# The turn of a slot's second-layer result placed between the two halves of the next slot's first-layer turn

## The chip, the cores and the metric

The kernel runs on one core of one Trainium2 chip. The metric is the device time of one execution in microseconds; the time shown for the kernel before is the median of 3 runs.

## The reference

Three residual blocks over x of 64 x 32 tokens with 256 channels: cross-attention to 257 context rows of 192 channels with 16 heads, local attention with a window of two tokens to each side, and a routed feed-forward part. The change touches the last one alone:

```python
router_logits = x @ Wr + br                       # 2048 tokens, 8 experts
expert_mask = one_hot(argmax(router_logits))      # one expert for each token
for e in range(8):
    h = gelu(x @ W1[e] + b1[e])                   # 256 -> 1024
    h = gelu(h @ W2[e] + b2[e])                   # 1024 -> 512
    y = h @ W3[e] + b3[e]                         # 512 -> 256
    out = out + expert_mask[:, e:e + 1] * y
```

## The kernel before

Both attention parts run over tiles of 128 tokens and end near 435 us. Then the tokens are sorted by expert into 23 slots of 128 rows (`SLOTS`), each slot with one expert, and each slot goes through three matrix layers. Every fp32 product is made of three products of rounded parts (`PRODUCTS`: high by high, high by low, low by high).

The work is written out for each engine, and semaphores join them. Each engine works its list in order. `over_slots` runs five slots straight, then a loop of three rounds of five slots, then the last three straight.

**PE**, for slot i (`slot`, L1810): layer 2 of slot i (24 matmuls, L1748), the turn of x for slot i+2 (2 transposes, L1687), the turn of z1 for slot i+1 (two halves of 4 transposes, L1728), the turn of z2 for slot i (4 transposes, L1756), layer 1 of slot i+2 (12 matmuls, L1696), layer 3 of slot i (13 matmuls, L1770 and L1762). z1 and z2 are the results of layers 1 and 2 with a token on each partition; a turn brings the channels onto the partitions, for the activation with its bias and for the next layer.

**ACT**, for slot i (`slot`, L958): copy of z2 from PSUM (`copy_z2`, L885), copies of the turned x (L870, L871), the second activation with its rounding for slot i (`second_layer`, L930 and L934; it waits for the turn of z2), the first activation with its rounding for slot i+1 in two halves (`first_layer`, L894 and L898; each half waits for its half of the turn of z1), the copies of z1 for slot i+2 (L876), the copy of y (L881). In the slot before the last, `first_layer_last` (L907, L911) comes ahead of `second_layer`.

**GpSimd (POOL)** makes the low parts: of x (L710), of the second layer's input (L717) and of the third's (L721); it also adds the residual (L727) and issues the gathers and scatters. **DVE** splits the weights into parts as they come in (L1336, L1339). **SP** issues their transfers, each as soon as the layer that reads the buffer's old contents has run for the last slot of its expert.

The waits around the change, on PE: the turn of z2 waits for `z2_copied` (ACT, L885) and `h2_hi_done`; each half of the turn of z1 waits for `z1_copied` (ACT, L876) and `h1_hi_done`; layer 2 waits for `h1_hi_done`, the rounding by L898, half by half. The halves of the turn of z1 go to the banks `ps_s[2]` and `ps_s[0]`, the turn of z2 goes to `ps_s[3]`, and layer 2 writes `ps_s[1]`.

Of the kernel before, what the change touches and what calls it, by code (L numbers as in the profile page):

```python
# [20 lines left out]
def perceiver_kernel(nc, x, ctx_turned, last_turned, mask, Wq, Wk, Wv, Wo, lWq_turned, lbq, lWk_turned, lbk, lWv, lbv,  # L21
# [30 lines left out]
    with ExitStack() as stack:  # L52
# [342 lines left out]
        def follows(i, n):  # L395

            return not isinstance(i, int) or i + n < SLOTS
# [7 lines left out]
        def is_last(i):  # L405
            return isinstance(i, int) and i == LAST
# [950 lines left out]
        def _(pe):  # L1357
# [58 lines left out]
            def keep_clock(n):  # L1416

                for _ in range(n):
                    t.transpose(ps_s[0][:, 0:P], ident[:, :], ident[:, :])
# [303 lines left out]
            def turn_z1_half(i, half):  # L1723
                pe.wait_ge(z1_copied, 2 * i + half + 1)
                pe.wait_ge(h1_hi_done, 2 * i)
                for c in range(4):
                    f = 4 * half + c
                    last = t.transpose(ps_t1[half][:, c * P:(c + 1) * P], z1[:, f * P:(f + 1) * P], ident[:, :])  # L1728
                last.then_inc(t1_filled, 1)

            def turn_z1(i):
                for half in range(2):
                    turn_z1_half(i, half)

            def layer2(i, e):
                pe.wait_ge(z2_copied, i)
                for products in (PRODUCTS[0:2], PRODUCTS[2:3]):
# [14 lines left out]
            def turn_z2(i):  # L1752
                pe.wait_ge(z2_copied, i + 1)
                pe.wait_ge(h2_hi_done, i)
                for c in range(F2 // P):
                    last = t.transpose(ps_t2[:, c * P:(c + 1) * P], z2[:, c * P:(c + 1) * P], ident[:, :])  # L1756
                last.then_inc(t2_filled, 1)
# [8 lines left out]
            def layer3_hi(i, e):  # L1766
                pe.wait_ge(w23_ready, 3 * e + 3)
                pe.wait_ge(h2_hi_done, i + 1)
                pe.wait_ge(y_copied, i)
                t.matmul(ps_y[:, 0:D], ones_r[:, :], b3_parts[:, bass.ds(e * D, D)], start=True, stop=False)  # L1770
                layer3_products(e, PRODUCTS[0:2], range(F2 // P))

            def layer3_lo(i, e):
                pe.wait_ge(h2_done, i + 1)
                layer3_products(e, PRODUCTS[2:3], range(F2 // P)).then_inc(y_filled, 1)
# [18 lines left out]
            def load_expert(i, q):  # L1794
                pe.reg_load(expert_in[q], slot_expert_int[0:1, bass.ds(i, 1)])

            def expert_of(q):
                return pe.snap(expert_in[q], min_val=0, max_val=E - 1)
# [11 lines left out]
            def slot(i, run, q):  # L1810
                expert = expert_of(q)
                layer2(i, expert)
                if is_last(i):
                    other = postponed.pop()
                    layer3_hi(i - 1, other)
                    turn_z2(i)
                    layer3_lo(i - 1, other)
                    keep_clock(8)
                    layer3_last(expert)
                    return  # L1820
                if follows(i, 2):
                    load_expert(i + 2, (q + 2) % AHEAD)
                    ahead = expert_of((q + 2) % AHEAD)
                    turn_x(i + 2, run + (q + 2) // AHEAD, (q + 2) % AHEAD)
                if follows(i, 1):
                    turn_z1(i + 1)
                turn_z2(i)
                if follows(i, 2):
                    layer1(i + 2, ahead)
                if last_but_one(i):  # L1830
                    postponed.append(expert)
                else:
                    layer3(i, expert)
# [38 lines left out]
```

## Time and profile before

| | |
|---|---|
| median of 3 runs | 742.54 us (741.34 to 744.79) |
| the profiled execution | 742.61 us |
| its span, first to last instruction | 740.9 us |
| mean granted TensorE clock | 0.987 |
| PE busy | 707.6 us, 96% |
| PE weight loads busy | 601.9 us, 81% |
| DVE busy | 470.0 us, 63% |
| ACT busy | 452.7 us, 61% |
| POOL busy | 422.7 us, 57% |

The share of the busy time is an average over parts of the kernel with different limits. Times in the rows further down are microseconds from the start of the span. PE stands for matmuls, PEld for the weight loads that run ahead of them; a transpose is a matmul too, with its load. The ends of matmuls are modelled, so PE can look busy while it waits, and the starts of the loads tell more.

### The profile page before, as it was taken

How to read it: one execution, taken by the hardware profiler on the slowest of the kernel's cores; microseconds unless marked ns; L12 is line 12 of the kernel's file. 1: busy time of each engine (PE TensorE's matmuls, PEld its weight loads, DVE VectorE, ACT ScalarE, POOL GpSimd, SP SyncE). 2: the span in 40 equal slices, each digit the busy share in tenths (PEclk: the TensorE clock that was granted, in tenths of full speed). 3: DMA queues.
4: the chain of work that ended last, by engine and by line, in shares of the span. 5: the costliest groups of instructions: out<-in, count | busy, mean ns of one | idle time of the engine just before them, and what ended most of it. 6: DMA issues, size and time to landing. Idle time of an engine off the chain costs nothing.

```text
span 740.9 us, 26310 instructions
## 1 busy us (share of the span) xinstructions
PE 707.6 (96%) x9211; PEld 601.9 (81%) x9212; DVE 470.0 (63%) x1381; ACT 452.7 (61%) x1073; POOL 422.7 (57%) x562
## 2 busy tenths in 40 slices
PE   8999999999999999999999848999999999997995
PEld 7888888888888888888888737887888888886884
DVE  4466677667776777777776569969923880288000
ACT  4666666666666666676666254565665757564654
POOL 6466656565565555555654104575757776675553
PEclk9999999999999999999999988999999999998999
DMA  7222332324232333334332903256026422271000
GB/s 219 89 79 83 82 89 78 92 65 105 78 90 66 79 96 83 80 74 92 86 81 95 341 29 100 93 180 223 22 100 211 145 79 78 86 256 36 21 7 1
DMA packets 55439, 73.92 MB, mean 100 GB/s; under 512 B 6269, under 2 KB 41118, under 8 KB 55392
## 3 DMA queue, kind: packets, MB, share of 16 engines
q1 hardware_dynamic: 49248, 60.36, 27.9%
q0 software_dynamic: 2944, 8.13, 3.6%
q10 hardware_dynamic: 3200, 4.80, 1.8%
q8 instruction: 29, 0.48, 0.3%
q14 instruction: 18, 0.15, 0.1%
HBM read 66.90 MB, written 7.27 MB: 100 GB/s over the span
## 4 chain that ended last, share of the span: by engine, by line
PE 84%; DVE 9%; DMA 3%; ACT 1%; issue 1%; POOL 0%; SPq 0%; POOLq 0%; ACTq 0%; DVEq 0%
PE ps_s L1748 15%; PE ps_kv L1366 11%; PE ps_kv L1374 11%; PE ps_p L1413 7%; PE ps_o L1399 6%; PE ps_s L1385 5%; DVE w L1339 3%; PE ps_kv L1696 3%; PE ps_p L1696 3%; PE ps_o L1762 3%; DVE w L1336 2%; PE ps_m L1512 2%; PE ps_m L1465 2%; PE ps_m L1444 2%; PE ps_s L1728 2%; PE ps_m L1517 2%
## 5 line engine op out<-in xcount | busy, mean ns | idle before, releaser
L1007 DVE CUSTOM_DVE_ANT_0 prob<-ps_s,mask_add 128x257 f32<-128x257 f32 x256 | 94.8, 422 | 66.8 <-PE ps_s L1385 66.8
L780 ACT ACTIVATE prob<-prob,neg_max 128x257 f32<-128x257 f32 x256 | 111.2, 500 | 41.7 <-DVE neg_max L1007 40.2
L1339 DVE TENSOR_TENSOR w<-w_raw,w 128x512 fp32r<-128x512 f32 x112 | 105.3, 943 | 3.7
L1336 DVE CAST w<-w_raw 128x512 fp32r<-128x512 f32 x94 | 63.4, 674 | 69.0 <-DMA w_raw<-in_L_ffn_W_dram 69.0
L612 POOL TENSOR_TENSOR ctx_parts<-ctx_raw,ctx_parts 128x512 fp32r<-128x512 f32 x64 | 82.8, 1293 | 31.5 <-ACT ctx_parts L775 30.5
L1748 PE MATMUL ps_s<-w,h_hi 128*128 x368 | 93.7, 406 | 7.2 <-DVE w L1339 5.9
L1748 PEld LDWEIGHTS ps_s<-w,h_hi 128*128 128x128 f32 x368 | 68.5, 191 | 25.5 <-issue 10.4
L1366 PE MATMUL ps_kv<-ctx_parts,wkv_hi 128*128 128x256 f32 x512 | 85.7, 295 | 0.2 <-POOL ctx_parts L612 0.2
L1374 PE MATMUL ps_kv<-wkv_hi,ctx_parts 128*128 128x256 f32 x512 | 84.9, 293 | 1.0 <-ACT kT L784 1.0
L717 POOL TENSOR_TENSOR h_lo<-h,h_hi 128x512 fp32r<-128x512 f32 x46 | 65.0, 1413 | 25.3 <-ACT h_hi L898 20.6
L788 ACT COPY v<-ps_kv 128x512 f32<-128x512 f32 x64 | 37.5, 585 | 66.6 <-PE ps_kv L1374 66.6
L1413 PE MATMUL ps_p<-ident,prob 128*128 128x128 f32 x512 | 77.0, 273 | 0.8 <-DVE probT L1029 0.8
L1366 PEld LDWEIGHTS ps_kv<-ctx_parts,wkv_hi 128*128 128x128 f32 x512 | 71.0, 191 | 2.3 <-issue 0.4
L1374 PEld LDWEIGHTS ps_kv<-wkv_hi,ctx_parts 128*128 128x128 f32 x512 | 69.4, 189 | 3.4 <-ACT kT L784 1.9
L605 POOL TENSOR_TENSOR ctx_raw<-ctx_raw,last_ctxT 128x512 f32<-128x512 f32 x64 | 69.4, 1085 | 1.3 <-DMA ctx_raw<-in_ctx_turned_dram 1.3
L1029 DVE COPY probT<-ps_p 128x512 f32<-128x512 f32 x64 | 44.1, 689 | 36.4 <-PE ps_p L1413 34.9
L885 ACT COPY lqk<-ps_s 128x512 f32<-128x512 f32 x23 | 13.5, 586 | 82.6 <-PE ps_s L1748 82.6
L1413 PEld LDWEIGHTS ps_p<-ident,prob 128*128 128x128 f32 x512 | 60.2, 141 | 2.9 <-DVE probT L1029 1.0
L625 POOL COPY last_prob<-prob 128x4 f32<-128x4 f32 x64 | 12.0, 187 | 87.7 <-ACT prob L780 80.6
L784 ACT COPY kT<-ps_kv 128x512 f32<-128x512 f32 x64 | 37.3, 582 | 28.0 <-PE ps_kv L1366 27.9
L894 ACT ACTIVATE h<-ps_s,bias_cols 128x128 f32<-128x128 f32 x176 | 50.1, 367 | 4.8 <-issue 3.9
L1399 PEld LDWEIGHTS ps_o<-v,probT 128*32 128x32 f32 x4096 | 41.0, 110 | 12.9 <-issue 12.6
(259 smaller groups left out, 1534.6 us busy)
## 6 DMA issues: line engine op xcount, KB each, us to landing
w_raw<-in_L_ffn_W_dram SPq DMA_DIRECT2D x24, 1024.0 KB, 7.8
ctx_raw<-in_ctx_turned_dram SPq DMA_DIRECT2D x63, 256.0 KB, 3.6
mask_add<-mask_dram SPq DMA_DIRECT2D x64, 128.5 KB, 3.4
rows_dram<-x3n ACTq DMA_DIRECT2D x16, 256.0 KB, 4.3
w_raw<-in_L_ffn_W_dram SPq DMA_DIRECT2D x8, 512.0 KB, 5.1
xt<-in_x_dram SPq DMA_DIRECT2D x16, 128.0 KB, 2.0
xr<-in_x_dram SPq DMA_DIRECT2D x16, 128.0 KB, 2.2
slot_x<-rows_dram,slot_ids POOLq DMA_INDIRECT x23, 3.7
```

What stands on the lines that cost most here:

```text
L605: g.tensor_tensor(ctx_raw[:, b, :, :], ctx_raw[:, b, :, :], last_ctxT[:, :, bass.ds(n, 1)].to_broadcast([P, 2, JM]), ALU.subtract).then_in ...
L612: g.tensor_tensor(ctx_parts[:, b % 2, 2:4, :], ctx_raw[:, b, :, :], ctx_parts[:, b % 2, 0:2, :].bitcast(F32), ALU.subtract).then_inc(split ...
L717: g.tensor_tensor(h1_parts[LO][:, fs, :], h1[:, fs, :], h1_parts[HI][:, fs, :].bitcast(F32), ALU.subtract).then_inc(h1_done, 1)
L780: a.activation(prob[:, g, :], prob[:, g, :], ACT.Exp, bias=neg_max[:, g:g + 1], scale=-1.0).then_inc(exp_done, 1)
L1007: d.tensor_tensor_reduce(prob[:, r, :], ps_s[r][:, 0:J], mask_add[:, k, :], -(HD ** -0.5), 3.0e38, ALU.add, ALU.min, neg_max[:, r:r + 1]). ...
L1336: d.tensor_copy(w[:, b, HI, part], raw[:, b, part]).then_inc(rounded, 1)
L1339: last = d.tensor_tensor(w[:, b, LO, part], raw[:, b, part], f32(w[:, b, HI, part]), ALU.subtract)
L1366: last = t.matmul(ps_kv[:, half * JM:(half + 1) * JM], w[:, 0, r, half * P:(half + 1) * P], ctx_parts[:, buffer, c, :], start=(i == 0), st ...
L1374: last = t.matmul(ps_kv[:, jt * D:(jt + 1) * D], ctx_parts[:, buffer, c, jt * P:(jt + 1) * P], w[:, 1, r, :], start=(i == 0), stop=(i == 4))
L1399: last = t.matmul(ps_o[h * S:(h + 1) * S, g * BLOCK:(g + 1) * BLOCK], probT[:, jt, g * P + h * S:g * P + (h + 1) * S], v[:, k % 2, jt, g / ...
L1413: last = t.transpose(ps_p[:, g * P:(g + 1) * P], prob[:, g, jt * P:(jt + 1) * P], ident[:, :])
L1748: last = t.matmul(ps_z2[:, :], h1_parts[hp][:, f, :], weight(w23, e % BUFFERS23, wp, f * F2, F2), start=(hp == HI and wp == HI and f == 0) ...
```

## The change

In PE's list for a slot, the turn of z2 of slot i moves up by four transposes: it now stands between the first and the second half of the turn of z1 of slot i+1. The function that did both halves in a row is dropped. The last slot and all other engines' lists stay as they are.

```diff
-            def turn_z1(i):
-                for half in range(2):
-                    turn_z1_half(i, half)
-
...
                 if follows(i, 1):
-                    turn_z1(i + 1)
+                    turn_z1_half(i + 1, 0)
                 turn_z2(i)
+                if follows(i, 1):
+                    turn_z1_half(i + 1, 1)
                 if follows(i, 2):
                     layer1(i + 2, ahead)
```

## Rows read from the trace of the kernel before

**Rows 1.** The page, chain that ended last, shares of the span by engine.

```profile
PE 84%; DVE 9%; DMA 3%; ACT 1%; issue 1%; POOL 0%; SPq 0%; POOLq 0%; ACTq 0%; DVEq 0%
```

**Rows 2.** Line L1756: its instructions, and who waited for it (us, times).

```profile
L1756 PEld LDWEIGHTS ps_s<-ident,lqk x92: 139/140/143, 466.6 to 730.5; 128*128 128x128 f32 x92
...
  ACT x3n L930: 12.7, 21
```

**Rows 3.** Order of time, PE's loads, one slot: start, us, what [idle before].

```profile
620.78 0.90 PEld L1728 LDWEIGHTS ps_s<-ident,prob 128*128 128x128 f32 x8
621.65 0.47 PEld L1756 LDWEIGHTS ps_s<-ident,lqk 128*128 128x128 f32 x4
622.09 0.77 PEld L1696 LDWEIGHTS ps_p<-w,xT_hi 128*128 128x128 f32 x4
...
623.37 0.89 PEld L1696 LDWEIGHTS ps_kv<-w,xT_hi 128*128 128x128 f32 x4
...
625.95 0.55 PEld L1762 LDWEIGHTS ps_o<-w,h_lo 128*128 128x128 f32 x4
626.65 0.52 PEld L1748 LDWEIGHTS ps_s<-w,h_hi 128*128 128x128 f32 x3 [0.16 <-issue]
```

**Rows 4.** Order of time, ACT, the same slot.

```profile
620.87 0.58 ACT L885 COPY lqk<-ps_s 128x512 f32<-128x512 f32 x1 [3.25 <-PE ps_s L1748]
...
622.59 1.14 ACT L930 ACTIVATE x3n<-ps_s,bias_cols 128x128 f32<-128x128 f32 x4 [0.58 <-PE ps_s L1756]
...
625.75 0.62 ACT L898 CAST h_hi<-h 128x512 fp32r<-128x512 f32 x1
```

**Rows 5.** Order of time: transposes behind a wait, and in a full stream.

```profile
455.66 0.60 ACT L876 COPY prob<-ps_p 128x512 f32<-128x512 f32 x1
...
456.31 0.42 PEld L1728 LDWEIGHTS ps_s<-ident,prob 128*128 128x128 f32 x4 [0.73 <-ACT prob L876]
...
456.32 0.66 PE L1728 MATMUL ps_s<-ident,prob 128*128 128x128 f32 x4 [0.29 <-ACT prob L876]
...
621.76 0.60 PE L1756 MATMUL ps_s<-ident,lqk 128*128 128x128 f32 x4
```

**Rows 6.** Order of time, PE's loads, a slot in which POOL held one up.

```profile
657.18 0.77 PEld L1696 LDWEIGHTS ps_p<-w,xT_hi 128*128 128x128 f32 x4
658.43 0.30 PEld L1696 LDWEIGHTS ps_p<-w,xT_lo 128*128 128x128 f32 x2 [0.48 <-POOL xT_lo L710]
658.77 0.88 PEld L1696 LDWEIGHTS ps_kv<-w,xT_hi 128*128 128x128 f32 x4
...
661.35 0.55 PEld L1762 LDWEIGHTS ps_o<-w,h_lo 128*128 128x128 f32 x4
661.82 0.31 PEld L1748 LDWEIGHTS ps_s<-w,h_hi 128*128 128x128 f32 x2
```

**Rows 7.** Order of time, ACT, a slot with a longer idle before L930.

```profile
540.14 1.14 ACT L930 ACTIVATE x3n<-ps_s,bias_cols 128x128 f32<-128x128 f32 x4 [0.87 <-PE ps_s L1756]
```

**Rows 8.** Order of time, PE's first loads of layer 2, outside the loop.

```profile
703.49 3.56 PEld L1748 LDWEIGHTS ps_s<-w,h_hi 128*128 128x128 f32 x16
...
715.08 1.00 PEld L1748 LDWEIGHTS ps_s<-w,h_hi 128*128 128x128 f32 x5
```

**Rows 9.** Order of time, ACT and PE's loads, into the last slot.

```profile
720.99 0.59 ACT L885 COPY lqk<-ps_s 128x512 f32<-128x512 f32 x1 [3.26 <-PE ps_s L1748]
...
723.07 0.39 PEld L1748 LDWEIGHTS ps_s<-w,h_hi 128*128 128x128 f32 x2 [1.02 <-issue]
```

**Rows 10.** The chain that ended last, in order of time: start, us, what.

```profile
644.21 5.55 DMA w_raw<-in_L_ffn_W_dram
...
680.05 5.96 PE ps_s L1748 x16
```

**Rows 11.** Busy time by stretch: us, each engine (instructions), granted clock, DMA share, GB/s.

```profile
511.00:580.00 69.00, 68.64 (x371) 57.96 (x371) 42.30 (x56) 43.45 (x122) 45.91 (x41) 1.00 0.31 103
676.00:680.00 4.00, 0.00 (x0) 0.00 (x0) 3.90 (x7) 0.14 (x1) 3.54 (x4) 0.70 0.10 32
680.00:686.00 6.00, 5.95 (x18) 4.69 (x19) 2.05 (x4) 0.00 (x0) 0.08 (x1) 0.63 0.10 31
```

## The prediction

> **What bounds the kernel now.** The page is read first: the chain that ended last is PE for most of the span [rows 1]. The change touches only the routed part, which starts near 450 us, so the views of that part come next. The list of who waits for the turn of the second-layer result shows 92 transposes, 23 slots of four, and that in 21 of the slots it is ACT that waits for them, before the activation at L930 [rows 2]. The order of time on PE's weight loads is then read over one slot, and the order of time on ACT over the same slot [rows 3, 4].
>
> The two together show a loop through both engines. Layer 2's first load comes at 614.96 in the slot before and 626.65 in this one, a period of 11.69 us (the first of these is one period ahead of the row shown). Inside it: the copy of z2 (L885) starts at 620.87, the activations of L930 at 622.59 after ACT was idle for 0.58 us on L1756, the first cast of L898 starts at 625.75 and ends at 626.37, and PE's load for layer 2 comes 0.28 us later, at 626.65, after 0.16 us of idle [rows 3, 4]. The same 0.28 us, give or take 0.02, stands between the end of that cast and this load in nearly every slot. So it is ACT that sets the period, by a little, while PE looks full.
>
> How little: in this slot the distance from the loads of layer 3's last product to layer 2's is 0.70 us (625.95 to 626.65) [rows 3]. In a slot in which PE had just been held up it is 0.47 us (661.35 to 661.82) [rows 6]. PE thus has 0.23 us of slack, and its own period would be 11.69 - 0.23 = 11.46 us.
>
> **The change, part by part.** Nothing is removed or added: the same twelve transposes of a slot run in another order, with the same waits. No DMA and no step of SP, POOL or DVE moves.
>
> *The turn of z2 comes earlier.* Its first load is at 621.65, after eight loads 0.11 us apart from 620.78 [rows 3]. With only four ahead it could start at 621.21. But it waits for the copy of z2, which ends at 620.87 + 0.58 = 621.45 [rows 4]. What the wait costs after that is in a place where PE waits for a copy of ACT: the copy ends at 455.66 + 0.60 = 456.26 and the load starts at 456.31, 0.05 us later [rows 5]. So the load starts at 621.50: 0.15 us earlier than now, and 0.29 us later than PE could take it. **A wait that the second half of the z1 turn covered until now is laid bare.**
>
> *What it costs PE.* The queue behind that wait is the second half of the z1 turn, then layer 1, layer 3 and layer 2 of the next slot. Not all of the 0.29 us is lost: four transposes that start on an idle array end 0.67 us after their first load (456.31 to 456.98), four in a full stream 0.71 us after (621.65 to 622.36) [rows 3, 5]. The stream behind moves by 0.29 - 0.04 = 0.25 us. The row gives 0.05 us for the wait.
> The Trainium skill (Advanced Engine Details and Errata, Network/Comms) gives 50 to 100 ns for the reading of a semaphore from a sequencer; the row is at its lower end. By its upper end, which no row here shows for this wait, the shift would be 0.30 us, and by that figure the sum would be about 0.8 us higher.
>
> *What it gives ACT.* The last transpose of z2 would end at 621.50 + 0.67 = 622.17 in place of 622.36, so L930 starts 0.15 us (by the loads) to 0.19 us (by the ends) earlier. ACT had been idle before it, so it can. All that follows on ACT, to the cast of L898, hangs on that start: ACT's part of the loop comes down to 11.50 to 11.54 us.
>
> *The second half of the z1 turn comes later:* its four loads came from 621.21, now they follow the four of z2, from about 622.0. Their reader is the second group of L894, which ACT starts only behind the cast of L898 at 625.75: over three us of cover. It costs nothing.
>
> *The two together.* PE's period becomes 11.46 + 0.25 = 11.71 us and ACT's 11.52. The larger decides: 11.71 against 11.69 now. **ACT's gain is real, and PE cannot take it, since the order that gives it spends PE's slack.** That PE's slack swallows such a delay is in the trace: a load held by POOL for 0.48 us moved the loads behind it from 1.28 us after layer 1's first (622.09 to 623.37) to 1.59 us after (657.18 to 658.77), so by 0.31 us, and the distance before layer 2 shrank from 0.70 to 0.47 us [rows 3, 6].
>
> *Where it counts.* 23 slots are turned. From 644.21 to 680.05 the chain runs through a weight transfer and DVE's rounding of it [rows 10]; three slots' turns lie beside it, and two more beside an earlier chain of that kind (489 to 511). The last two slots have other chains. 23 - 5 - 2 = 16 count. Twelve of them are in the loop of the program. In nine the period is like the one above: 9 x 0.02 = +0.2 us. In three ACT is late for a reason of its own, as at 540.14, where it had been idle for 0.87 us in place of 0.58 [rows 7]; there PE waits for longer than its slack and most of the 0.15 us is taken: 3 x 0.12 = -0.35 us. Four stand outside the loop, where ACT loses less before L894 and the period is down to 11.59 us (703.49 to 715.08) [rows 8]: PE's 11.71 costs up to 0.12 us there, estimated at 0.09 on average, +0.35 us. A POOL hold at layer 1 and the new stall don't add, since the later of the two decides.
> *The last slot.* There is no turn of x ahead; the copy of z2 starts at 720.99 and PE stands idle for 1.02 us before layer 2 at 723.07 [rows 9]. A turn of z1 that is 0.44 us later fits in there: nothing.
>
> Sum: +0.2 - 0.35 + 0.35 = +0.2 us. The profiled execution took 742.61 us with a span of 740.9; the median of the three runs is 742.54. **Forecast: 742.8 us,** the execution's 742.61 and the sum. What a measurement of this kernel can tell from no change is about 0.5%, or 3.7 us.
>
> **The rivals.**
> *PE's stall is paid in full (slower).* One mechanism at one place: the load of z2 waits at the head of PE's queue, and PE's slack of 0.23 us before layer 2 is not slack. Against it: the slack comes from the difference of two distances, and the held slot at 658.43. For it: PE is reported idle for only 0.16 us at that place, not 0.23 [rows 3]. With the stall paid in full, 16 x 0.25 = 4.0 us, 746.6. It turns into a loss as soon as the stall exceeds the slack by 0.02 us a slot; it would be beyond 0.5% only with nearly nothing absorbed. With 0.16 us of slack, it is 16 x 0.09 = 1.4 us, 744.0.
> *ACT's gain comes through (faster).* If the stream behind moves by far less than 0.25 us, because the loads behind catch up, ACT stays the bound and the full 0.15 us a slot is gained: 16 x 0.15 = 2.4 us, 740.1. For it: of the 0.48 us hold only 0.31 came through, so streams do catch up [rows 6]. Against it: the four transposes behind a wait of the same kind got back only 0.04 us [rows 5].
> *The clock.* PE's granted clock was 1.00 over 511 to 580 although each slot has 14 transposes, and 0.63 over 680 to 686, after PE had run nothing from 676 to 680 [rows 11]; 16 matmuls took 5.96 us there where their loads otherwise take 3.56 [rows 8, 10]. If the new gap of 0.3 us among the transposes brought such a fall once or twice, the cost is some 2 us each: 745 to 747.
> The Trainium skill (TensorE: Matmul & The Clock Gate, Part 4: PE-mode transpose) says that transposes do not count as work for the clock gate, which would make a gap among them worse than one elsewhere; the trace's 1.00 over whole slots speaks against it deciding here. By it the time would be that of the rows, 745 to 747.
> *The change does nothing,* because the copy's end and not the order sets the z2 turn already: excluded by 621.45 against 621.65.
>
> **How the numbers follow.** Forecast case (PE and ACT about level, within 1.5 us of now) 0.74; ACT's gain comes through 0.11; the stall is paid in part or in full 0.11, of which a third beyond 0.5%; the clock 0.04. Range 740.2 to 745.8: the lower end is the full gain of ACT, the upper one is most of a stall paid. Faster by over 0.5%: 0.03 (2.4 us plus luck with the clock at 680). Slower by over 0.5%: 0.07. Within 0.5%: 0.90.
>
> **What would show it.** In the changed kernel: the first load of L1756 0.05 us after the end of L885, PE idle there by about 0.2 to 0.3 us with ACT as the releaser; ACT's idle before L930 down from 0.58 to about 0.40; no idle before L1748's first load; the period 11.7. If the period is 11.55 the catch-up was under-rated, if it is above 11.8 the slack was over-rated. A clock below 1.00 between 511 and 644 would make the prediction wrong.

## The result, and the profile after

The changed kernel takes 740.72 us in the median of 18 runs (739.81 to 742.13), the kernel before 742.42 us in 18 runs beside them (739.17 to 745.66). The ratio is 0.9979, with an interval of 0.9969 to 0.9989. So the change gains 1.7 us, 0.2%. The forecast was a loss of 0.2 us. The time lies inside the forecast's range, but it moved in the direction that had got little weight, and the reasons have to be looked at one by one.

The profiled execution of the changed kernel took 740.58 us, with a span of 738.8 against 740.9. The page's head, its first row of engines and the chain that ended last, which answers [rows 1]:

```profile
span 738.8 us, 26310 instructions
PE 708.2 (96%) x9211; PEld 600.4 (81%) x9212; DVE 472.1 (64%) x1381; ACT 453.1 (61%) x1073; POOL 425.7 (58%) x562
PE 88%; DVE 7%; DMA 1%; ACT 1%; issue 1%; POOL 0%; SPq 0%; POOLq 0%; ACTq 0%; DVEq 0%
```

The share of DVE in that chain fell from 9% to 7% and that of DMA from 3% to 1%. Rounded as they are, that is some 15 us of a chain at least that left the path (the one of slot 4, from 489 to 511, is such a chain). The change touches neither engine. This row is the first hint of where the gain is.

In the code of the changed kernel the lines behind L1730 are four lower: L1748 is L1744 now, L1756 is L1752, L1762 is L1758. The turn of z2, the view that answers [rows 2]:

```profile
L1752 PEld LDWEIGHTS ps_s<-ident,lqk x92: 138/140/144, 466.3 to 728.4; 128*128 128x128 f32 x92
...
  ACT lqk L885: 6.1, 23
...
  ACT x3n L930: 8.6, 21
```

ACT waits for these transposes for 8.6 us in place of 12.7, and PE now waits 6.1 us for the copy of z2, 0.26 us a slot on average. The same slot as in [rows 3, 4], in the order of time: PE's loads, then ACT.

```profile
618.80 0.47 PEld L1728 LDWEIGHTS ps_s<-ident,prob 128*128 128x128 f32 x4
619.52 0.42 PEld L1752 LDWEIGHTS ps_s<-ident,lqk 128*128 128x128 f32 x4 [0.26 <-ACT lqk L885]
619.91 0.47 PEld L1728 LDWEIGHTS ps_s<-ident,prob 128*128 128x128 f32 x4
620.35 0.76 PEld L1696 LDWEIGHTS ps_p<-w,xT_hi 128*128 128x128 f32 x4
...
624.20 0.54 PEld L1758 LDWEIGHTS ps_o<-w,h_lo 128*128 128x128 f32 x4
624.66 2.41 PEld L1744 LDWEIGHTS ps_s<-w,h_hi 128*128 128x128 f32 x11
```

```profile
618.88 0.59 ACT L885 COPY lqk<-ps_s 128x512 f32<-128x512 f32 x1 [3.46 <-PE ps_s L1744]
...
620.41 1.15 ACT L930 ACTIVATE x3n<-ps_s,bias_cols 128x128 f32<-128x128 f32 x4 [0.39 <-PE ps_s L1752]
...
623.58 0.62 ACT L898 CAST h_hi<-h 128x512 fp32r<-128x512 f32 x1
```

The load of z2's turn comes 0.05 us after the copy's end (618.88 + 0.59 = 619.47, then 619.52). L930 starts 1.53 us after the copy's start, where it was 1.72. The distance from layer 3's last product to layer 2 is 0.46 us (624.20 to 624.66), where it was 0.70: PE's slack is used up. And the load of layer 2 comes 0.46 us after the end of the cast (624.20), where it was 0.28: **ACT now runs about 0.2 us ahead of PE at the start of layer 2 in most slots** (in a few it has no lead, in some 0.4 us), where PE was right behind ACT before.

So this slot is as forecast. The first loads of layer 2 give a ledger of the slots (before, after):

| first load of layer 2 | before | after | difference | gained between |
|---|---|---|---|---|
| slot 4 | 507.12 | 507.13 | +0.01 | |
| slot 5 | 520.47 | 518.83 | -1.64 | -1.65 in slot 4 |
| slot 16 | 650.06 | 648.08 | -1.98 | -0.34 in slots 5 to 15 |
| slot 18 | 673.49 | 671.76 | -1.73 | +0.25 in slots 16 and 17 |
| slot 19 | 691.82 | 689.57 | -2.25 | -0.52 in slot 18 |
| slot 22 | 723.07 | 721.00 | -2.07 | +0.18 in slots 19 to 21 |

Four fifths of the difference come from one slot. PE's loads of layer 2 in slot 4, first of the kernel before, then of the changed one:

```profile
507.12 1.69 PEld L1748 LDWEIGHTS ps_s<-w,h_hi 128*128 128x128 f32 x8
510.71 1.69 PEld L1748 LDWEIGHTS ps_s<-w,h_hi 128*128 128x128 f32 x8 [1.90 <-issue]
```

```profile
507.13 3.57 PEld L1744 LDWEIGHTS ps_s<-w,h_hi 128*128 128x128 f32 x16
```

Before, PE stopped for 1.90 us in the middle of layer 2. After, the 16 loads run through. What PE waits for there is the second half of W2 of the third expert. Its path: when layer 2 of slot 2 has run (the *trigger*, the start of L885 in that slot, 489.38 before, 489.46 after), SP issues the transfer, and DVE splits the two pieces of W2 into high and low parts in 16 operations (L1336 and L1339 in turn). PE is ready for the second half 19.3 to 19.5 us after the trigger in every kernel below. In the kernel before DVE was done at +21.20, in the changed one at +19.34.

The second place is slot 18, which waits for the last expert's W2. The granted clock there, in the changed kernel, answers [rows 11] (columns: us, PE, PEld, DVE, ACT, POOL busy, granted clock, DMA share, GB/s):

```profile
511.00:580.00 69.00, 68.88 (x373) 57.43 (x372) 43.32 (x55) 45.49 (x126) 47.60 (x41) 1.00 0.33 105
676.00:680.00 4.00, 1.78 (x5) 1.43 (x6) 3.86 (x8) 0.00 (x0) 1.94 (x2) 0.81 0.30 78
680.00:686.00 6.00, 5.98 (x30) 4.85 (x29) 0.28 (x1) 1.84 (x6) 0.73 (x1) 0.84 0.00 0
```

From that slot's trigger (end of layer 2 in slot 15) to the end of DVE's splitting it is 35.7 to 35.8 us in both kernels, so the order gains nothing there. But layer 2 of slot 18 ends 41.5 us after the trigger in place of 41.8, and that of slot 19 starts 47.27 us after it in place of 47.61. Around the end of the stop the granted clock is at the lower of its two levels (1.2 GHz, half) for a while. By these rows and [rows 11] it is (0.19 x 4 + 0.16 x 6) / 0.5 = 3.4 us in the profile of after and (0.30 x 4 + 0.37 x 6) / 0.5 = 6.8 us in that of before. The 6.8 us began some 2.4 us before PE went on at 680.04 (the mean clock was 0.90 over 676 to 678 and 0.50 over 678 to 680).

### The profile page after: what moved, and what is told of

Read it like the earlier page. It is cut to its first block, busy times and chain, and to the rows that moved or that the text cites. A ratio compares the mean times of both kernels' runs of the same rounds, so it can differ in the third digit from the quotient of the medians.

```text
span 738.8 us, 26310 instructions
## 1 busy us (share of the span) xinstructions
PE 708.2 (96%) x9211; PEld 600.4 (81%) x9212; DVE 472.1 (64%) x1381; ACT 453.1 (61%) x1073; POOL 425.7 (58%) x562
## 4 chain that ended last, share of the span: by engine, by line
PE 88%; DVE 7%; DMA 1%; ACT 1%; issue 1%; POOL 0%; SPq 0%; POOLq 0%; ACTq 0%; DVEq 0%
PE ps_s L1744 16%; PE ps_kv L1366 11%; PE ps_kv L1374 11%; PE ps_p L1413 7%; PE ps_o L1399 6%; PE ps_s L1385 5%; PE ps_p L1696 4%; PE ps_kv L1696 4%; PE ps_o L1758 4%; PE ps_s L1728 2%; DVE w L1339 2%; PE ps_m L1512 2%; PE ps_m L1465 2%; PE ps_m L1444 2%; PE ps_m L1517 2%; PE ps_s L1752 2%
## 5 line engine op out<-in xcount | busy, mean ns | idle before, releaser
L1336 DVE CAST w<-w_raw 128x512 fp32r<-128x512 f32 x94 | 70.8, 753 | 65.4 <-DMA w_raw<-in_L_ffn_W_dram 65.4
L1339 DVE TENSOR_TENSOR w<-w_raw,w 128x512 fp32r<-128x512 f32 x112 | 99.9, 895 | 3.7
L1744 PE MATMUL ps_s<-w,h_hi 128*128 x368 | 91.9, 401 | 4.8 <-DVE w L1339 4.3
L1744 PEld LDWEIGHTS ps_s<-w,h_hi 128*128 128x128 f32 x368 | 68.3, 190 | 20.9 <-issue 6.3
L717 POOL TENSOR_TENSOR h_lo<-h,h_hi 128x512 fp32r<-128x512 f32 x46 | 64.5, 1403 | 27.3 <-ACT h_hi L898 22.4
L885 ACT COPY lqk<-ps_s 128x512 f32<-128x512 f32 x23 | 13.5, 586 | 84.5 <-PE ps_s L1744 84.5
L1399 PEld LDWEIGHTS ps_o<-v,probT 128*32 128x32 f32 x4096 | 41.0, 110 | 12.9 <-issue 12.6
```

The lines of the kernel that those rows point to most:

```text
L717: g.tensor_tensor(h1_parts[LO][:, fs, :], h1[:, fs, :], h1_parts[HI][:, fs, :].bitcast(F32), ALU.subtract).then_inc(h1_done, 1)
L1336: d.tensor_copy(w[:, b, HI, part], raw[:, b, part]).then_inc(rounded, 1)
L1339: last = d.tensor_tensor(w[:, b, LO, part], raw[:, b, part], f32(w[:, b, HI, part]), ALU.subtract)
L1399: last = t.matmul(ps_o[h * S:(h + 1) * S, g * BLOCK:(g + 1) * BLOCK], probT[:, jt, g * P + h * S:g * P + (h + 1) * S], v[:, k % 2, jt, g / ...
L1744: last = t.matmul(ps_z2[:, :], h1_parts[hp][:, f, :], weight(w23, e % BUFFERS23, wp, f * F2, F2), start=(hp == HI and wp == HI and f == 0) ...
```

## The experiments

All kernels of this part, those of the order of before and those of the changed order, read the expert's number on PE with stated bounds in place of a plain load of the register:

```diff
-                pe.reg_load(expert_in[q], slot_expert_int[0:1, bass.ds(i, 1)])
+                pe.reg_mov(expert_in[q], pe.value_load(slot_expert_int[0:1, bass.ds(i, 1)],
+                                                       min_val=0, max_val=E - 1))
```

The expectations name theories by letters, and the quoted texts say what each expects. In short: A, the forecast's account, by which the loop is level and what remains is the clock behind slot 18's stop; B, the loop itself gains; C, the stop in slot 4 makes it; D, the weight transfer of slot 4 collides with GpSimd's gather and scatter around the trigger; E, it is how DVE's splitting alternates with GpSimd's work; F, a sharper form of C, by which the lead of ACT and GpSimd over PE at the trigger decides how often PE has to stop.

**Both orders once more.** First the kernel before and the changed one with only the edit above.

> The kernel before, with one thing added: PE loads the expert's number with its bounds asserted (as ACT does), which the experiments with edits need too. It is the base of the experiments. Theory A (the gain lies in when the weights of one expert arrive): the slots in which no weights are waited for have a period near 11.70 us, and the stop of PE before the second half of layer 2 in slot 4 (1.65 us in the trace of before) is there again, though its size may differ from run to run. Theory B (the gain lies in the loop of PE and ACT itself): the same periods, but the stop in slot 4 has no part in the difference to the changed order. Both: a time within 0.5 us of the kernel before, 742.4 us.

> The changed kernel with the same added assertion on PE. Theory A: the plain slots have 11.70 to 11.72 us again, not less than in the base, and slot 4 has no stop or a clearly shorter one; 1 to 2 us faster than the base. Theory A2 (as A, but the arrival of the weights is a matter of chance in each execution): slot 4 may show a stop here as well, and the difference to the base is under 1 us. Theory B: the plain slots are shorter than in the base by 0.1 us each.

Measured: 742.30 us (741.06 to 743.51, 11 runs) and 741.36 us (740.46 to 745.57, 12 runs), against 742.39 of the kernel before (23 runs); ratios 0.9998 (0.9987 to 1.0010) and 0.9987 (0.9975 to 1.0000). No cost of the edit can be seen. Between the two medians lie 0.9 us, in the direction of the gain, but with 11 and 12 runs that is not quite clear of nothing (95% interval from resampling the runs: a loss of 0.1 to a gain of 1.5 us). What these two taught was in their profiles. The order of before had a stop in slot 4 of only 0.18 us this time (profiled run 741.37 us), and the changed order had one of 1.68 us (742.09 us):

```profile
506.43 1.69 PEld L1748 LDWEIGHTS ps_s<-w,h_hi 128*128 128x128 f32 x8 [0.22 <-issue]
508.35 1.70 PEld L1748 LDWEIGHTS ps_s<-w,h_hi 128*128 128x128 f32 x8 [0.23 <-issue]
```

```profile
507.00 1.73 PEld L1744 LDWEIGHTS ps_s<-w,h_hi 128*128 128x128 f32 x8
510.46 1.70 PEld L1744 LDWEIGHTS ps_s<-w,h_hi 128*128 128x128 f32 x8 [1.72 <-issue]
```

So **the stop is not fixed by the order: in either order it can be short or about 1.7 us long.** Profiles further down confirm it for programs that are the same up to slot 4: the order of before has 0.18 us here and 1.89 us in the pair on slot 18, the changed order 1.68 us here and 0.06 us with the first five slots changed. What the order can change is how often.

**No weights to wait for.** The transfers and the splitting of the weights are left out from the fourth expert on for the first layer and from the third on for the others. Later slots then work with the matrices of earlier experts, and no slot waits for weights. DVE signals the buffers as ready by copies of one column.

```diff
             for first_matrix, e in LATE:
+                if e >= (3 if first_matrix else 2):
+                    continue
...
```

> The order of before; the transfers and the splitting of the weights of the later experts (third W1 buffer onward and all W2 and W3 behind the first two experts) are left out, so part of the computation uses the weights of earlier experts, and no slot waits for weights. What is left is PE with ACT and POOL. Both theories: some 6 us or more below the kernel before, since the stops of slots 4 and 18 go (1.65 and 6.6 us). Theory A: about level with its counterpart in the changed order. Theory B: 1.5 to 2 us above it.

> The changed order with the same parts of the weights' transfers and splitting left out. Theory A: within 0.5 us of the order of before without weights, rather above it than below (11.71 against 11.69 and 11.60 us a slot). Theory B: 1.5 to 2 us below it.

Measured: 733.74 us (733.29 to 734.27) and 733.78 us (733.69 to 734.32), four runs each. The medians are level to 0.04 us. With four runs each that holds to some 0.5 us, so the gain of 1.7 us sits on the waits for weights, little or none of it in the loop as such, and theory B fell. The spread of a kernel is at most 1 us here; with the weights it is 1.6 to 6.5 us, in more runs.

**Slot 4 without its wait.** The transfer and the splitting of the third expert's W2 and W3 are left out, and its slots 4 to 8 work with the first expert's matrices.

```diff
             for first_matrix, e in LATE:
+                if not first_matrix and e == 2:
+                    continue
...
```

> The base in the order of before; the transfer and splitting of W2 and W3 of the third expert are left out, so its slots 4 to 8 use the first expert's matrices, and slot 4 waits for no weights. Slot 18's stop stays. Theory A (plain slots level, the gain in the arrival of weights in slot 4 and in the clock after the stop in slot 18): 0 to 1 us below the base, and 0.5 to 1 us above its counterpart in the changed order. Theory C (only slot 4's stop makes the difference): level with its counterpart within 0.3 us.

> The changed order with the same left out. Theory A: 0.5 to 1 us below its counterpart in the order of before, with TensorE at half clock for 3.4 us after slot 18's stop where the order of before has 6.8 us. Theory C: level with it.

Measured: 740.89 us (739.66 to 742.11) and 741.06 us (740.60 to 742.19), 12 runs each, against 742.48. Level: 0.17 us the other way, known to some 0.7 us. Taking the stop away gains 1.4 us in the order of before (from 742.30) and 0.3 in the changed one (from 741.36), which has most of it already; the 0.3 alone is within the noise. Theory C held. The half-clock stretch at slot 18 is still in both kernels, 6.8 us in the profile of the first and 3.4 us in that of the second, and the medians are level all the same. That speaks against the part of theory A that puts the gain there.

**Slot 18 without its wait.** The same for the last expert's W2 and W3 (`e == 7`); its slots 18 to 22 work with the sixth expert's.

> The base in the order of before; the transfer and splitting of W2 and W3 of the last expert are left out (its slots 18 to 22 use the sixth expert's), so that PE does not stop in slot 18 and the clock does not fall there. Slot 4 may stop. Theory A: 6 to 8 us below the base, and above its counterpart by less than 0.8 us (what slot 4 makes). Theory C: above its counterpart by the full 1 to 1.7 us.

> The changed order with the last expert's W2 and W3 left out. Theory A: within 0.8 us of its counterpart, since the clock has no part here. Theory C: 1 to 1.7 us below it.

Measured: 735.75 us (734.16 to 736.79, 6 runs) and 734.80 us (734.32 to 736.03, 5 runs). A difference of 0.95 us remains without slot 18's stop, as large as in the first pair. So few runs can't tell it from nothing (95% interval: a loss of 0.4 to a gain of 1.8 us), and it lies just under theory C's 1 to 1.7 and just over theory A's 0.8. (Both profiles happen to show the long stop in slot 4, 1.89 and 1.75 us.) The stop in slot 18 costs 6 to 7 us in either order.

**The way cleared for the transfer.** GpSimd's gather for slot 5 and scatter of slot 1 are moved away from the trigger.

```diff
-                if i + 3 < SLOTS:
+                if i + 3 < SLOTS and i != 2:
                     gather_slot(i + 3)
-                if i > 0:
+                if i > 0 and i != 2:
                     scatter_slot(i - 1)
...
+                if i == 1:
+                    gather_slot(5)
+                if i == 2:
+                    scatter_slot(1)
```

> The base in the order of before; POOL issues the gather of slot 5 one slot earlier (behind the low part of slot 1's second-layer result), and the scatter of slot 1 behind the low part of slot 2's, so that neither is on its way when the third expert's W2 is called for at the end of slot 2's layer 2. Theory D (slot 4's stop comes from this transfer sharing the DMA engines with a gather and a scatter issued 1.9 and 0.3 us ahead of it; the changed order lets ACT and POOL lead PE by 0.2 to 0.4 us and so frees the way): the transfer lands after 5.5 to 5.9 us, not 6.9 to 7.4; the stop is under 0.3 us; 1 to 1.5 us below the base. Theory E (the stop comes from how DVE's splitting alternates with POOL's work, not from the transfer): the landing may be earlier, the stop stays in most executions; level with the base.

> The changed order with the same move of one gather and one scatter. Theory D: level with e9 within 0.4 us, and 0 to 0.6 us below the changed order, since its stop, where it still comes, goes too. Theory E: 0.8 to 1.5 us below e9, as without the move.

Measured: 744.84 us (742.21 to 745.70, 11 runs) and 744.57 us (742.55 to 746.11, 10 runs), ratios 1.0021 (1.0009 to 1.0033) and 1.0022 (1.0011 to 1.0033): slower than the kernel before (742.41) by 2.4 and 2.2 us in the medians. Neither theory had expected that; D had expected 1 to 1.5 us less and E no change for the first. The two are level with each other, as D had said. The first half of theory D came true as well: the first piece landed at +5.42 and +5.62 us in place of +7.26. But DVE was done later, at +21.8 and +22.2, and the stops in slot 4 were 2.6 and 2.9 us. The trace of the order of before with the way cleared, DVE and then GpSimd, shows why:

```profile
495.74 0.43 DVE L1340 CAST w<-w_raw 128x512 fp32r<-128x512 f32 x1 [3.77 <-DMA w_raw<-in_L_ffn_W_dram]
496.20 4.01 DVE L1343 TENSOR_TENSOR w<-w_raw,w 128x512 fp32r<-128x512 f32 x1
500.14 0.41 DVE L1340 CAST w<-w_raw 128x512 fp32r<-128x512 f32 x1
```

```profile
495.36 1.02 POOL L735 DMA_INDIRECT out_dram<-y,slot_ids  x1 [0.16 <-issue]
496.41 2.56 POOL L717 TENSOR_TENSOR h_lo<-h,h_hi 128x512 fp32r<-128x512 f32 x2
498.94 0.72 POOL L727 TENSOR_TENSOR y<-y,slot_x 128x256 f32<-128x256 f32 x1
```

The moved scatter held GpSimd up, so its two L717 and L727 came back to back. One DVE operation that otherwise takes 0.69 us lasted 4.01 us, until 0.55 us after the end of that row (499.66). That is theory E's point: an operation of DVE that meets one of GpSimd waits for its end, here for the whole row, which had no gap.

**GpSimd made later in the changed order.** One copy of 128x128 more ahead of the gather for slot 5.

```diff
+                if i == 2:
+                    g.tensor_copy(band_shifted[:, :], band[:, :])
                 if i + 3 < SLOTS:
                     gather_slot(i + 3)
```

> The changed order; POOL makes one copy of 128 x 128 more (some 0.5 us) ahead of the gather of slot 5, which takes away its lead there. Theory D: gather and scatter go out as late as in the order of before, the third expert's W2 lands 0.5 to 1.5 us later than in the changed order on average, and the time goes up by about 1 us to 742.2. Theory E: level with the changed order within 0.4 us.

Measured: 741.45 us (739.98 to 743.37, 12 runs), ratio 0.9987 (0.9977 to 0.9997), the same as without the copy (741.36). The scatter started 0.09 us before the trigger in place of 0.87, and the transfer still landed at +5.75. So the place of gather and scatter alone doesn't decide, and theory D, which had expected 742.2, fell.

**PE made later in the order of before,** once, by three transposes ahead of layer 2 of slot 2. ACT and GpSimd then have the lead that the changed order gives them, at this one trigger.

```diff
                                     pe.wait_ge(h1_hi_done, 2 * i + half + 1)
+                                    if isinstance(i, int) and i == 2 and hp == HI and half == 0:
+                                        for _ in range(3):
+                                            t.transpose(ps_s[3][:, 0:P], ident[:, :], ident[:, :])
```

> The base in the order of before; three transposes more on PE (0.3 us) ahead of slot 2's layer 2, so that this one trigger comes 0.3 us later against ACT and POOL, as it does in the changed order. Theory D: the stop of slot 4 gets rarer or shorter; 0.3 us paid, about 1 won: 0.5 to 0.9 us below the base. Theory E: 0 to 0.3 us above the base.

Measured: 741.58 us (740.73 to 743.33, 11 runs), ratio 0.9992 (0.9983 to 1.0000). **With work that does nothing put on the busiest engine, the median is 0.7 us lower** than that of its counterpart without it (742.30), as theory D had expected; the interval of the ratio just reaches no change, so this is support and not proof. PE's loads into slot 2 and in slot 4:

```profile
482.86 0.35 PEld L1750 LDWEIGHTS ps_s<-ident 128*128 128x128 f32 x3
483.18 1.00 PEld L1751 LDWEIGHTS ps_s<-w,h_hi 128*128 128x128 f32 x5
...
506.69 1.70 PEld L1751 LDWEIGHTS ps_s<-w,h_hi 128*128 128x128 f32 x8 [0.27 <-issue]
509.00 1.69 PEld L1751 LDWEIGHTS ps_s<-w,h_hi 128*128 128x128 f32 x8 [0.61 <-issue]
```

The stop is 0.6 us. The comparison is across two groups of runs, each against its own runs of the kernel before (742.39 and 742.41).

**The order changed in some slots only.** Five straight slots at the start alone, and then all slots but these (with the opposite condition in the first line).

```diff
+                apart = isinstance(i, int) and i < AHEAD
                 if follows(i, 1):
                     turn_z1_half(i + 1, 0)
+                    if not apart:
+                        turn_z1_half(i + 1, 1)
                 turn_z2(i)
-                if follows(i, 1):
+                if follows(i, 1) and apart:
                     turn_z1_half(i + 1, 1)
```

> The changed order in the five straight slots at the start alone (slots 0 to 4); the loop of three rounds and the last three slots have the order of before. Theory F (what the change gives is all in the stop of layer 2 in slot 4, and that hangs on how far ACT and POOL lead PE when the weight transfer is triggered, at the end of slot 2's layer 2): the whole difference is here, so 741.0 to 741.4 us against 742.4 of the kernel before, ratio 0.9981 to 0.9987; the outer slots at the end then keep their old period, which is worth another 0.2 us. In the profile the lead before slot 2's layer 2 is 0.45 us or more (0.28 before). Theory A (the loop and the clock at slot 18 make it): level with the kernel before, 742.2 to 742.5.

> The counterpart: slots 0 to 4 have the order of before, the loop and the last three slots have the changed one. Theory F: nothing of the gain is left, 742.2 to 742.7 us, ratio 0.9997 to 1.0004, since the stop of slot 4 is that of the kernel before in most executions. Theory A: 741.0 to 741.5 us, the gain is all here. If both kernels of this pair gain about half, neither theory holds alone.

Measured: 741.53 us (740.69 to 743.89) and 742.99 us (741.61 to 744.74), 12 runs each, against 742.49 (29 runs); ratios 0.9990 (0.9978 to 1.0001) and 1.0008 (0.9997 to 1.0020). The first has as much of the gain as the whole change showed in this kind of kernel (741.36), though its interval just includes no change. It is 0.1 us above theory F's bracket. The second has none of the gain: it is 0.5 us above the kernel before and 0.3 above the bracket, which theory F doesn't explain. The two are 1.5 us apart, in the same group of runs (95% interval: 0.6 to 2.3 us), which is clear of the noise. Theory A had expected it the other way round. So **the gain is made in the first five slots, although most slots are among the rest.** PE's loads of layer 2 in slot 4, the first five slots alone and the rest alone:

```profile
507.28 3.56 PEld L1744 LDWEIGHTS ps_s<-w,h_hi 128*128 128x128 f32 x16
```

```profile
507.23 1.70 PEld L1744 LDWEIGHTS ps_s<-w,h_hi 128*128 128x128 f32 x8
510.99 1.70 PEld L1744 LDWEIGHTS ps_s<-w,h_hi 128*128 128x128 f32 x8 [2.06 <-issue]
```

The first kernel was also the candidate for beating both, since its last slots keep the shorter period. It doesn't, as far as can be told: an advantage of 0.2 us can't be seen here.

**ACT made later in the changed order,** the mirror of the three transposes: copies ahead of the cast of the first half of slot 2's first layer, two of 128x64 and then, since these were too few, five of 128x24.

```diff
+                    if isinstance(i, int) and i == 2 and half == 0:
+                        for at in (0, P // 2):
+                            a.copy(band_shifted[:, at:at + P // 2], band[:, at:at + P // 2])
                     act.wait_ge(gelu1_done, 2 * i + half + 1)
```

> The changed kernel with two copies of 128x64 more on ACT ahead of the cast of the first half of slot 2's first layer, some 0.45 us in all: ACT and POOL lose their lead over PE at the one place where the weight transfer for slot 4 is about to be triggered. The mirror of the run with three transposes more on PE. The added work itself costs PE 0.45 less the lead of 0.2, so 0.25 us. Theory F: the lead is gone there, the stop in slot 4 comes back to that of the kernel before, 742.2 to 742.7 us, layer 2 of slot 4 held by 1.7 to 1.9 us in the profile. Without an effect of the lead: 741.3 to 741.7 us (about 741.2 and 0.25), with a stop that is most often near 0.1 us.

> The run before it with a larger dose, since two copies of 128x64 held ACT up by 0.15 us only (cast of the first half at 482.28 in place of 482.13) and left most of the lead, 0.56 of 0.71 us: now five copies of 128x24, some 0.14 us each, 0.55 us of ACT's time beyond what they hide. PE's load for layer 2 of slot 2 is then released by that cast, 0.28 us behind it as in the kernel before, and all the rest of the kernel moves by 0.1 to 0.2 us. Theory F: no lead is left at the trigger, layer 2 of slot 4 is held by 1.7 to 2.0 us in most executions, 742.3 to 742.9 us. If the lead at that one trigger has no effect and only the sequence of PE's work has: 741.4 to 741.8 us and a stop that is near 0.1 us.

Measured: 742.11 us (740.95 to 743.15) with two copies, 742.92 us (740.87 to 744.88) with five, 12 runs each, against 742.49 (29 runs) and 742.14 (17 runs); ratios 0.9997 (0.9985 to 1.0009) and 1.0015 (1.0000 to 1.0030). With two, the lead shrank by 0.15 us to 0.55 us, and the profile shows no stop; the time falls between the brackets of theory F (742.2 to 742.7) and of no effect (741.3 to 741.7). With five, ACT and then PE read, in order of time:

```profile
482.36 0.67 ACT L899 COPY band_shifted<-band 128x24 f32<-128x24 f32 x5
482.91 0.64 ACT L901 CAST h_hi<-h 128x512 fp32r<-128x512 f32 x1
```

```profile
483.83 1.23 PEld L1747 LDWEIGHTS ps_s<-w,h_hi 128*128 128x128 f32 x6
...
510.74 1.70 PEld L1747 LDWEIGHTS ps_s<-w,h_hi 128*128 128x128 f32 x8 [1.70 <-issue]
```

PE's load comes 0.28 us behind the cast (483.55), so the lead is gone, and the stop of 1.7 us is back. The direction and the profile are theory F's. The size is not clean: it is 0.8 us above the kernel before, where theory F puts it about level, and in both of these kernels layer 2 of slot 17 was held for 1.38 us in the middle, and the weights for slot 18 came 0.7 to 0.8 us later after their trigger than in most others. Of the other profiles only one shows such a hold in slot 17 (changed order, way cleared, 1.90 us); the rest have 0.3 us or less. Why an edit in slot 2 should do that isn't known; it may be a second wait with two outcomes. Of the 1.6 us by which five copies are above the changed order (741.36), up to 0.8 belongs to that.

**What decides in slot 4.** The first load of layer 2 in slot 2 after the end of the cast (the lead; 0.28 is none), the landing of the first piece (the start of DVE's first operation on it) and the end of DVE's 16 operations after the trigger, and the stop, by one profile of each kernel:

| kernel | lead | landed | DVE done | stop |
|---|---|---|---|---|
| before | 0.29 | 7.26 | 21.20 | 1.86 |
| before, again | 0.28 | 6.89 | 19.51 | 0.18 |
| before, slot 18 without wait | 0.28 | 7.40 | 21.24 | 1.89 |
| changed in the rest alone | 0.28 | 7.09 | 21.36 | 2.01 |
| changed, ACT late by five copies | 0.28 | 7.12 | 20.87 | 1.66 |
| changed, ACT late by two | 0.55 | 6.43 | 19.21 | 0.06 |
| changed, again | 0.56 | 6.74 | 20.82 | 1.68 |
| before, PE late | 0.58 | 6.79 | 19.78 | 0.57 |
| changed | 0.70 | 5.78 | 19.34 | 0.06 |
| changed, GpSimd late | 0.71 | 5.75 | 19.34 | 0.06 |
| changed in the first five alone | 0.71 | 5.87 | 19.34 | 0.06 |
| changed, slot 18 without wait | 0.73 | 7.32 | 21.00 | 1.75 |
| before, way cleared | 0.53 | 5.42 | 21.82 | 2.64 |
| changed, way cleared | 0.70 | 5.62 | 22.23 | 2.91 |

(The stop counts from where PE would have been ready, so it is up to 0.05 us from the idle time in the row.) Leave aside the two with the way cleared, where GpSimd's work was moved. Then, without a lead, the stop is long in four profiles of five, and with one of 0.7 us it is absent in three of four. That looks like a shift of odds and not like a switch, and nine profiles are too few to call the odds measured. The landing sorts the stops better than the lead does: all five at +7.09 or later have the long stop, all four up to +6.43 have none, and of the three between (+6.74 to +6.89) each is different. DVE's part of the path varies as well, 12.6 to 14.3 us for the same 16 operations. How DVE and GpSimd meet in the kernel before, first DVE, then GpSimd:

```profile
507.32 1.54 DVE L1336 CAST w<-w_raw 128x512 fp32r<-128x512 f32 x1
508.90 1.68 DVE L1339 TENSOR_TENSOR w<-w_raw,w 128x512 fp32r<-128x512 f32 x1
```

```profile
506.91 3.12 POOL L717 TENSOR_TENSOR h_lo<-h,h_hi 128x512 fp32r<-128x512 f32 x2 [0.51 <-ACT h_hi L898]
```

And in the changed kernel:

```profile
504.94 1.66 DVE L1339 TENSOR_TENSOR w<-w_raw,w 128x512 fp32r<-128x512 f32 x1
506.52 0.41 DVE L1336 CAST w<-w_raw 128x512 fp32r<-128x512 f32 x1
506.97 1.82 DVE L1339 TENSOR_TENSOR w<-w_raw,w 128x512 fp32r<-128x512 f32 x1
```

```profile
504.73 1.33 POOL L721 TENSOR_TENSOR h_lo<-x3n,h_hi 128x512 fp32r<-128x512 f32 x1 [1.17 <-ACT h_hi L934]
506.92 1.32 POOL L717 TENSOR_TENSOR h_lo<-h,h_hi 128x512 fp32r<-128x512 f32 x1 [0.87 <-ACT h_hi L898]
```

A cast takes 0.42 us and a subtraction 0.69 when nothing meets them, and 1.5 to 1.8 when they start beside an operation of GpSimd: the subtraction at 506.97 ends at 508.79, 0.55 us after L717's end at 508.24. In the changed profile this subtraction was the 16th and last operation, so PE went on at 508.93. In that of before the chain had started 1.5 us later, its last two operations fell beside both L717, and they ended at 510.58. The steps of such a path are whole operations of GpSimd, which would explain why the stop is short or 1.7 us and only once between (0.57).
The Trainium skill (SBUF — State Buffer, Who interferes with whom) says that VectorE and GpSimd share a pair of ports by an exclusive lock: a VectorE instruction in a two-port mode, or one with two inputs in SBUF beside a GpSimd instruction that reads SBUF, and the GpSimd instruction can't run side by side, and whichever comes first holds the ports to its end while the other blocks. The rows agree, with the 4.01 us operation as the plainest.

## Why the prediction was right or wrong, point by point

**What bounds the kernel: right.** ACT set the period by a little, and PE's slack was 0.23 us: the distance before layer 2 shrank by just that, 0.70 to 0.46 us.

**The bare wait: right.** 0.05 us from the copy's end to the load, and 0.26 us of idle for a forecast of 0.29.

**What it gives ACT: right.** 0.15 to 0.19 us forecast, 0.19 measured (1.72 to 1.53).

**The two together: right.** The period was forecast at 11.71 us; most slots of the loop have 11.70 or 11.72. Outside the loop it rose from 11.59 to 11.72, in two rows that answer [rows 8]:

```profile
701.27 3.58 PEld L1744 LDWEIGHTS ps_s<-w,h_hi 128*128 128x128 f32 x16
...
712.99 3.11 PEld L1744 LDWEIGHTS ps_s<-w,h_hi 128*128 128x128 f32 x14
```

**The sum over the slots that were counted: right.** By their times, the turns that the prediction counted are those of slots 0, 1, 4, 5 to 14 and 18 to 20. By the first loads of layer 2 (in slots 4 and 18 only what lies behind the stop), slots 5 to 14 together take 117.55 us for 117.82, and the twelve in the loop give -0.23 us for the -0.15 forecast, and the four outside +0.42 for +0.35. That is +0.19 us together for +0.2. The slot of [rows 7], with ACT late, gained 0.14 (11.97 to 11.83), and ACT's idle there fell from 0.87:

```profile
538.27 1.14 ACT L930 ACTIVATE x3n<-ps_s,bias_cols 128x128 f32<-128x128 f32 x4 [0.68 <-PE ps_s L1752]
```

The last slot, of [rows 9], has 8.01 us for 7.99.

**Where it counts: this step failed.** It took three slots beside the weight chain of [rows 10] and "two more beside an earlier chain of that kind (489 to 511)" out of the sum, and so put what ends these chains at nothing. The two profiles have -1.7 us for layer 2 of slot 4 and -0.5 us for layer 2 of slot 18, out of -2.1 us in all. For the chain at 644 the arrival was indeed the same, 35.7 to 35.8 us from trigger to DVE's end in both orders. What is gained from that trigger to layer 2 of slot 19, 0.34 us, goes with the shorter stretch at half clock (see below); the forecast had counted none of it. For the one at 489 it was wrong. Its end is not given but falls mostly in one of two places 1.7 us apart, and with the order of the first five slots the time moves. The prediction counted the transfer's trigger as unmoved since it hangs on PE. It said that no step of DMA, SP, GpSimd or DVE moves. It did not ask what stands beside the chain's engines: GpSimd, whose operations hold up those of DVE, follows ACT, and ACT gained 0.2 us on PE. The prediction even had the number (ACT 11.52, PE 11.71), and wrote it off as a gain that PE cannot take.

That most of the gain is that stop follows from taking it away (level to 0.17 us), from the order in the first five slots alone (the gain) and in the rest alone (none). That the lead of ACT at the trigger is what matters is supported, not shown: from one side by PE made later (0.7 us less, at the edge of the noise), from the other by ACT made later, with a side effect that blurs the size. How the lead would make the transfer land earlier stays open. The table has it so mostly, 5.8 us against 7.1, but the place of gather and scatter alone doesn't explain it, and there is an exception at 7.32.

**The rivals.** ACT's gain in full (740.1) comes nearest the time (740.72) and is wrong in its mechanism: with no waits for weights the orders are level to 0.04 us. PE's stall paid in full didn't happen. The clock stayed at 1.00 from 511 to 580, and up to 644, in spite of the gap among the transposes, so neither the row nor the rule on transposes led to the 745 to 747 us. The clock at slot 18 did vary, 6.8 or 3.4 us at half, worth some 0.3 to 1.2 us from the trigger to the end of slot 18's layer 2 (41.4 to 41.5 in place of 41.8 to 42.7). It is part of why the two profiles differ by 2.1 us where the medians differ by 1.7.

The clock remains a rival for a part of the gain. In the order of before the long stretch is in all four profiles that have slot 18's stop and GpSimd's order as it was, and in the changed order in three of six, two of them with ACT made late. The mean granted clock of single runs points the same way: of the 125 runs of the kernel before beside the experiments, 50 have a mean of 0.983 or less and take 743.1 us on average, where the other 75 take 741.9; of the 18 runs of the changed kernel none is below 0.985. Against a large part stands the pair without slot 4's wait: 6.8 and 3.4 us by its profiles, and level medians. Whether the stop in slot 4 and the length of that stretch hang together was not tested.

**The range held the time, the sign was missed.** That the time lies inside is luck: the lower end, 740.2, was drawn from ACT's gain in full, which did not come. The sum went by one profiled execution, in which the stop was long, as it is in four of the five profiles without a lead. A forecast that had asked whether the 1.90 us would stay would have had a case of its own: some 1.6 us at most, 741.0, as an estimate from that row.

## What to carry to other kernels

When a change shifts one engine against another without moving the bound, look for the rare waits behind the slots that are left out of the sum, and follow every engine that their path shares something with; a stop that is there in some executions only is worth its whole length times the change of its odds. One profile can't show such a stop's odds: compare the same slot in several profiled executions before a length read from one is taken as given. And take a wait away in both kernels: if they become level, it was that wait, whatever the loop looks like.

## What the runs showed of the hardware that was not expected

- An operation of DVE beside one of GpSimd waits for its end: 0.42 and 0.69 us became 1.5 to 1.8 us, and one took 4.01 us beside two L717 and an L727 in a row. Sixteen operations that take 8 x (0.45 + 0.61) = 8.5 us alone took 12.6 to 16.6 us.
- The same transfer, issued at the same place, landed 5.4 to 7.4 us after its trigger (5.8 to 7.4 with GpSimd's order as it was).
- With three idle transposes on the busiest engine, 0.3 us of work, the median was 0.7 us lower, at the edge of the noise.
- The stretch at half clock around the end of one and the same stop, 4.7 to 4.9 us long in most profiles, was 3.4 or 6.8 us long. In the profile of before it began some 2.4 us before the stop ended.
